# Softmax denominators of an attention and recurrence kernel: one group of four sums per two head pairs, divisors spread by transfers

## What is computed

```python
xn = _layernorm(x)
qkv = xn @ W_qkv + b_qkv                       # 16 heads of 64
scores = einsum('nqhd,nkhd->nhqk', q, k)
attention = softmax(scores / sqrt(64), axis=3)
out = einsum('nhql,nlhd->nqhd', attention, v).reshape(n, l, 1024) @ W_out + b_out
c = f * c + i * g                              # a gated recurrence over the 8 batches, on xn
h = tanh(xn @ wo.T + c_final @ uo.T + bo)
return x + out + h
```

## Time and profile before

| | |
|---|---|
| median of 3 runs | 908.32 us (907.5 to 911.02) |
| the profiled execution: its own time | 911.83 us |
| its span | 910.0 us |
| granted TensorE clock, mean | 0.979 |
| busy: PE, DVE, POOL, ACT | 96%, 63%, 60%, 49% |

### The profile page before, as it was taken

One profiled execution on the slowest core, in us unless ns is written; L12 is line 12 of the kernel. 1 busy time (PEld: TensorE's weight loads), 2 busy tenths in 40 slices (PEclk: granted clock), 3 DMA queues, 4 the chain that ended last, 5 costly groups with the idle time before them and its releaser, 6 DMA issues.

```text
span 910.0 us, 14933 instructions
## 1 busy us (share of the span) xinstructions
PE 875.1 (96%) x5429; PEld 554.0 (61%) x5429; DVE 571.1 (63%) x770; ACT 444.7 (49%) x579; POOL 548.2 (60%) x270
## 2 busy tenths in 40 slices
PE   4779999999999999999999999999999999999988
PEld 3545655655666666665666566665666566666643
DVE  6856666664766556665667476664766476665632
ACT  4335645652555555552555455552555355553531
POOL 4024644644777667773777677773777577774764
PEclk9669999999999999999999999999999999999999
DMA  7000000000100000000100000000100000000000
GB/s 232 1 0 1 9 17 0 1 13 1 36 2 13 0 1 34 0 12 0 35 0 12 0 23 12 0 12 0 35 0 12 0 23 12 0 13 1 13 13 12
DMA packets 18635, 13.75 MB, mean 15 GB/s; under 512 B 1298, under 2 KB 16176, under 8 KB 18608
## 3 DMA queue, kind: packets, MB, share of 16 engines
q1 hardware_dynamic: 18608, 13.39, 4.7%
HBM read 6.83 MB, written 2.10 MB: 10 GB/s over the span
## 4 chain that ended last, share of the span: by engine, by line
PE 89%; DVE 6%; ACT 2%; DMA 1%; issue 1%; SPq 1%; DVEq 0%
PE st L747 20%; PE pv L761 12%; PE misc L761 12%; PE st L689 9%; PE mx L728 8%; PE st L753 6%; PE mx L777 6%; PE mx L771 6%; PE pv L689 2%; DVE NM L507 2%; PE misc L673 2%; PE misc L689 2%; DMA probs<-in_L_attn_data_dram 1%; ACT probs L360 1%; DVE KL L493 1%; PE pv L673 1%
## 5 line engine op out<-in xcount | busy, mean ns | idle before, releaser
L507 DVE TENSOR_REDUCE NM<-mx 128x2 f32<-128x1024 f32 x256 | 313.8, 1226 | 172.7 <-PE mx L728 172.7
L360 ACT ACTIVATE probs<-st 128x1024 f32<-128x1024 f32 x256 | 257.3, 1027 | 93.9 <-PE st L753 88.7
L251 POOL TENSOR_TENSOR AT<-AT,RD 128x512 f32<-128x512 f32 x63 | 80.8, 1282 | 231.9 <-DVE RD L525 171.1
L259 POOL TENSOR_TENSOR PSUMK<-probs 128x1024 f32<-128x1024 f32 x64 | 153.4, 2397 | 99.5 <-ACT probs L360 99.5
L265 POOL TENSOR_TENSOR PSUMK<-PSUMK,probs 128x1024 f32<-128x1024 f32 x64 | 152.9, 2389 | 6.1
L272 POOL TENSOR_TENSOR PSUMK<-PSUMK,probs 128x1024 f32<-128x1024 f32 x64 | 152.8, 2387 | 6.1
L761 PE MATMUL misc<-probs,VALL 128*64 128x512 f32 x512 | 129.1, 593 | 0.9 <-DVE DL L472 0.9
L761 PE MATMUL pv<-probs,VALL 128*64 128x512 f32 x512 | 124.8, 607 | 0.7 <-DVE RES L478 0.7
L728 PE MATMUL mx<-KH,QH 64*128 64x512 f32 x512 | 112.4, 435 | 9.8 <-DVE NM L507 8.8
L747 PE MATMUL st<-QH,KH 64*128 64x512 f32 x512 | 107.4, 415 | 0.8 <-ACT probs L360 0.6
L747 PE MATMUL st<-QL,KH 64*128 64x512 f32 x512 | 101.5, 392 | 0.0
(11 more groups left out here) (179 smaller groups left out, 1240.5 us busy)
## 6 DMA issues: line engine op xcount, KB each, us to landing
probs<-in_L_attn_data_dram SPq DMA_DIRECT2D x4, 512.0 KB, 7.6
XSH<-XH SPq DMA_DIRECT2D x8, 256.0 KB, 2.4
XSL<-XL SPq DMA_DIRECT2D x8, 256.0 KB, 2.4
RES<-in_L_attn_data_dram SPq DMA_DIRECT2D x8, 256.0 KB, 2.8
out_dram<-RES SPq DMA_DIRECT2D x8, 256.0 KB, 2.3
probs<-in_L_attn_W_qkv_dram SPq DMA_DIRECT2D x3, 512.0 KB, 4.7
MROW<-TM SPq DMA_DIRECT2D x64, 4.0 KB
WO<-in_L_attn_W_out_dram SPq DMA_DIRECT2D x1, 512.0 KB, 4.8
```

The costliest lines, as they stand in the source:

```text
L251: nc.gpsimd.tensor_tensor(AT[:, s % PAIRS, :], AT[:, s % PAIRS, :], RD[:, s % 2, :], ALU.mult).then_inc(norm_done, 1)
L259: nc.gpsimd.tensor_tensor(PSUMK[:, s % 2, :, :], e[:, :, 0, :], e[:, :, 1, :], ALU.add).then_inc(sum_part, 1)
L360: nc.scalar.activation(probs[:, s % 2, :, u, :], st[:, u % 2, :, :], ACT.Exp, scale=SCALE).then_inc(exp_done, 1)
L507: nc.vector.tensor_reduce(NM[:, 0:4 * TB].rearrange("p (h a b) -> p h a b", h=2, a=2)[:, :, s % 2, b], mx[:, :, :], AX.X, ALU.max, negate= ...
```

## The change

- `sums` is called once per step, for both pairs. It makes four matmuls of 32 columns (`tile_position=(0, g)`), one head each in 32 partitions of the bank `st[:, 1, 1, :]`, and stands behind the second pair's values, in front of the next step's first maxima. In the last step it stands in front of the second pair's values. It waits for the POOL sums of both pairs and for DVE's `lo_k`, which reads that bank.
- DVE transposes the four heads' sums once into `RD[:, 0]` and takes one reciprocal into `R16`.
- SP copies the 16 columns of `R16` by six transfers into `RX`, so that each head's divisors stand in its 64 partitions, for both pairs.
- DVE fills `RD` from `RX` with one spreading transpose per pair in the next step, behind the fifth and the sixth of the eight reductions; the last step's fills come after its transfers.
- POOL normalises both pairs of the step before between its sums for the first and the second pair of the present one; before, one stood at the front and one at the end.
- PE no longer waits for the divisors' transpose before a step's first maxima, but before the scores of the first pair's second block, which use `st[:, 1]`.

```diff
+        RX = sb("RX", [P, 2, L // 32])
...
+            def spread_divisors(n, j):
+                sp.wait_ge(r16_done, STRETCHES * n + j + 1)
+                sp.sem_inc(passed_sp, 1)
+                for a in range(2):
+                    for to, of, count in ((0, 0, 32), (32, 0, 64), (96, 32, 32)):
+                        sp.dma_start(RX[to:to + count, a, :],
+                                     R16[HD * a + of:HD * a + of + count, :]).then_inc(d_r, 16)
...
                     for k in range(2):
-                        first_sum(t + k, s + k)
+                        first_sum(n, j, t + k, s + k)
                         second_sum(t + k, s + k)
                         third_sum(t + k, s + k)
-                    normalise(t, s)
+                        if k == 0 and not (first and j == 0):
+                            normalise(t - 2, s - 2)
+                            normalise(t - 1, s - 1)
...
+            def divisors(n, j):
+                dve.wait_ge(den_done, STRETCHES * n + j + 1)
+                wait(dve, norm_done, 8 * n + 2 * j)
+                nc.vector.transpose(RD[:, 0, :], st[:, 1, 1, :]).then_inc(den_used, 1)
+                dve.wait_ge(den_used, STRETCHES * n + j + 1)
+                wait(dve, d_r, 96 * (STRETCHES * n + j))
+                nc.vector.reciprocal(R16[:, :], RD[:, 0, :].rearrange("p (c j) -> p c j", j=32)[:, :, 0]).then_inc(r16_done, 1)
+            def fill_divisors(n, j, a):
+                dve.wait_ge(d_r, 96 * (STRETCHES * n + j + 1))
+                nc.vector.transpose(RD[:, a, :].rearrange("p (c j) -> p c j", j=32),
+                                    RX[:, a, :].unsqueeze(2).to_broadcast([P, L // 32, 32])).then_inc(rd_done, 1)
...
+            def sums(t):
+                pe.wait_ge(sum_done, t + 2)
+                for a in range(2):
+                    for h in range(2):
+                        g = 32 * (2 * a + h)
+                        last = nc.tensor.matmul(st[g:g + 32, 1, 1, :], ones[:, 0:32], PSUMK[:, a, h, :], start=True,
+                                                stop=True, tile_position=(0, g))
                 last.then_inc(den_done, 1)
...
-                    if coming:
-                        pe.wait_ge(red_done, 4 * (t + 4))
-                    sums(t, s, mx[:, 1, :])
...
                     pe.wait_ge(exp_done, 4 * t + 8)
+                    if not coming:
+                        sums(t)
+                    values(n, t + 1, s + 1)
                     if coming:
-                        values(n, t + 1, s + 1, (0, 1))
-                        pe.wait_ge(tm_done, STRETCHES * n + j + 2)
-                        sums(t + 1, s + 1, mx[:, 0, :])
-                        values(n, t + 1, s + 1, (2, 3))
-                    else:
-                        sums(t + 1, s + 1, st[:, 0, 0, :])
-                        values(n, t + 1, s + 1)
+                        if ahead:
+                            pe.wait_ge(k_lo, t + 6)
+                        sums(t)
```

More of the change, by code:

```diff
@@ L252, in normalise, with first_sum @@
                                         ALU.mult).then_inc(norm_done, 1)
-            def first_sum(t, s):
+            def first_sum(n, j, t, s):
                 pool.wait_ge(exp_done, 4 * t + 2)
-                wait(pool, den_done, t - 1)
+                wait(pool, den_done, STRETCHES * n + j)
                 e = probs[:, s % 2, :, :, :]
@@ L277, in step @@
                     s, t = 2 * j, 8 * n + 2 * j
-                    if not (first and j == 0):
-                        normalise(t - 1, s - 1)
                     for k in range(2):
-                        first_sum(t + k, s + k)
+                        first_sum(n, j, t + k, s + k)
                         second_sum(t + k, s + k)
                         third_sum(t + k, s + k)
-                    normalise(t, s)
+                        if k == 0 and not (first and j == 0):
+                            normalise(t - 2, s - 2)
+                            normalise(t - 1, s - 1)
             batches(pool, step)
+            normalise(8 * N - 2, PAIRS - 2)
         @block.scalar
@@ L605, in step @@
                     if coming:
-                        for b in range(TB - 1):
-                            maxima(t + 3, s + 3, b)
+                        maxima(t + 3, s + 3, 0)
+                    if not (first and j == 0):
+                        fill_divisors(n, j - 1, 0)
+                    if coming:
+                        maxima(t + 3, s + 3, 1)
+                    if not (first and j == 0):
+                        fill_divisors(n, j - 1, 1)
+                    if coming:
+                        maxima(t + 3, s + 3, 2)
                     if first:
@@ L627, in step @@
                         lo_state(s + 2)
[L628 to L629 removed]
+                    divisors(n, j)
             batches(dve, step)
+            fill_divisors(N - 1, 3, 0)
+            fill_divisors(N - 1, 3, 1)
             dve.wait_ge(pv_done, 8 * N)
@@ L857, in step @@
                         pe.wait_ge(tm_done, STRETCHES * n + j + 1)
-                        wait(pe, den_used, t)
+                        if first:
+                            wait(pe, t_done, 3 * s - 1)
+                        elif j == 1:
+                            pe.wait_ge(o_evac, n)
                         score_maxima(t + 2, s + 2, 0)
@@ L863, in step @@
                     if first:
+                        wait(pe, den_used, STRETCHES * n + j)
                         scores(n, t, s, 1, (0, 1, 2))
```

17 lines of the change are left out of this document (2 added, 15 removed).

## The result

| | before | after |
|---|---|---|
| median of the timed runs beside each other, us | 909.76 (906.76 to 911.49, 10 runs) | 914.68 (912.43 to 915.41, 10 runs) |
| profiled execution's span, us | 910.0 | 913.1 |
| granted clock, mean over the span | 0.979 | 0.975 |

The changed kernel is slower: the ratio is 1.0057, with a 95% interval from 1.0041 to 1.0073. The forecast was 0.8% slower.

The account below looks back on a forecast made before the run. PE, busy 96% of the span, was taken as the bound; steps -6.2 and +0.6, first batch +2.4 and tail +10.2 gave +7.0 us, so 915.3 against the 908.32 median, 0.8% slower, range 900 to 924.

Parts of the forecast that it names:

- Sums, "I take 0.86": PE's one group of four sums per step costs 0.86 us, plus 0.15 for tile-shape switching; gain 0.71 per step.
- two at a time: Rival on PE's sums: four strips run two at a time, the group takes 1.72 us, total 943; chance 6%.
- the estimate of 1.08: Rival on PE's sums: four strips cost 1.08 us and not 0.86, 7 us more, total 922; chance 8%.
- The first maxima, "loss 0.36 per step, say 0.4": At each seam PE's second maxima wait for DVE's late first reduction: 0.25 us plus 0.11 of open weight load.
- j = 1, "loss about 0.4, seven times": In later j = 1 steps the second pair's values wait for DVE's residual addition, no longer covered by sums.
- First batch, +2.4: First batch's four steps lose 0.15 us each, its three seams 0.6 each, since removing the first sums gains nothing there.
- the switch: Extra PE entry into and exit from the sums' tile shape, put at 0.15 us per step, between 0 and 0.3.
- POOL hides "by 0.3 to 0.7": POOL's sums and two normalisations end 20.9 us into the step, before PE asks, with 0.3 to 0.7 spare.
- Transfers: SP's six divisor copies take 4.1 us to issue, land after 5.5, and are hidden in the next step.
- Tail, +10.2: Last step grows 10.2 us: product wait 2.9, switch 0.15, half clock 0.8, late divisors 4.5, further clock and transposes 1.9.
- Sum: Whole execution: ordinary steps -6.2, j = 1 steps +0.6, first batch +2.4, tail +10.2, together +7.0 us.
- The late reduction costs nothing: Rival at the seams: DVE's late first reduction does not delay PE; steps of 22.2 us, total 902.7; chance 22%.

Follow-up runs that it names:

- The last kernel: Changed kernel plus reciprocal behind the first reduction, earlier residual addition, last step's old divisors and reordered values, product and sums; 892.32 us, ratio 0.9804 to the kernel before.

## Why the prediction was right

The sign, the size (0.8% forecast, 0.57% measured) and the range held, and the likeliest case was the one that came: one cheap group, a first reduction that comes late, and a long tail. The mechanisms are shown by the experiments. That the size fits so well is in part luck, since several terms were off in both directions. By its steps:

- *Sums, "I take 0.86".* Right. The group is one row of eight records in two bunches 0.45 apart (0.48 foreseen), and costs 0.99 up to the next maxima (1.01 foreseen). The last kernel shows the whole gain with the losses removed: 0.64 to 0.79 a step, 0.71 foreseen. The two rivals in which four strips cost more (two at a time, or the estimate of 1.08 from the Trainium skill, "TensorE: Matmul & The Clock Gate", section on packing small matmuls) would have made it 1.85 or 1.21. This trace shows no price for the third and the fourth strip.
- *The first maxima, "loss 0.36 per step, say 0.4".* The mechanism is right, and that the second maxima wait for DVE is shown by doubling and by moving the reciprocal. The size was off both ways. At the written-out seams it is 0.22: the sum had the reduction start at 1.15 and last 1.23, and it started at 1.06 and lasted 1.17, since it begins 0.08 before the reciprocal's record ends. At the loop's own seam it is 0.77: the gap of 0.42 on DVE was not foreseen. In the kernel before, the last instruction there was a spreading transpose of 0.7 us, which covered it, and the change left a reciprocal of 0.25 in its place. The mean over a looped batch, (3 x 0.22 + 0.77) / 4 = 0.36, is the number that was worked out, by two errors that cancel in this mean.
- *j = 1, "loss about 0.4, seven times".* Right: with the residual addition earlier, 0.35 came back.
- *First batch, +2.4.* Measured +2.1, but not by its terms. The second pair's values do wait the 0.86 more that the first sums covered (1.09 and not 0.23). The late reduction was put at 0.6 at each of three seams; moving the reciprocal gave back 0.20 to 0.27 there, so it was put at more than twice its price. What remained, 0.27 to 0.30 a step, is twice the 0.15 that was put for the switch, and no run shows why. The seam into the loop, measured +0.59, had only 0.15 in this term, and 0.42 of it was the reciprocal.
- *POOL hides "by 0.3 to 0.7".* It hides by 0.8. The run with the sums between the values shows how little that is: asked 1.9 earlier, POOL's chain is what PE waits for.
- *Transfers.* Hidden in the steps: the six are issued from 449.40 in the step from 448.16, and the first fill starts at 457.68, directly behind a reduction. Six issues take 3.76 and not 4.1, and in the last step the fill starts 4.85 after the first issue (897.07 to 901.92), where 5.5 was put.
- *Tail, +10.2.* Measured +10.7 for the last step itself. The product came 2.7 late and not 2.9, its half clock cost 1.7 where half of that (0.8) was put, and the end product came 9.20 after the sums, where 9.8 was put.
- *Sum.* +7.0 was forecast on the profiled execution, and the spans differ by 3.1. Of the missing 3.9, 1.3 is the start's scatter, 0.3 the first batch, and 2.8 the ends of the 27 later steps, for which the sum had -5.6 and the marks show -8.4 (-7.8, and -0.6 in front of the last step); the tail gives 0.5 back. The term that was mis-sized there is "say 0.4", which counts 27 x 0.4 = 10.8. What was lost is 20 x 0.22 at the written-out seams, 5 x 0.77 at the loop's and 0.36 at its exit, 8.6 in all; the 27th seam leads into the last step, which has no maxima to delay. An ordinary step is 22.47 long, below the forecast's 22.6 to 22.7 and above the rival's 22.2.
- *"The late reduction costs nothing".* The rival had no share. Its condition, DVE free before 0.9 into the step, is met only with the reciprocal behind the first reduction, where the reduction starts 0.78 to 0.83 into the step, and there an ordinary step is what the rival had said (22.27, against its 22.2).

What stays open: why a written-out seam loses 0.22, the loop's exit 0.36 and the way into the loop 0.42 with the same instructions. At the first, the reduction's record begins 0.08 before the reciprocal's ends; at the other two it begins behind it, and its length is 1.23 and not 1.17. That accounts for the difference, but no run shows what makes it. Open is also what the first batch's steps lose beside the reciprocal.

## What to carry to other kernels

When work on the bounding engine moves to the end of a step, look at what its reader has queued in front of that engine's next need: here a reciprocal of 0.25 us in the wrong place cost a third of the gain at a written-out seam and all of it at the loop's own, and moving it behind one reduction gave that back. Let the last instruction before a loop's branch be a long one on an engine that is awaited right behind it; that was seen on DVE here, and on no other engine. Merge work in the steady state and keep the old form in the last step, where a latency that other steps hide stands in the open: the last step cost 10.7 us here, against the 8.4 that all step ends behind the first batch gained.

## What the runs showed of the hardware

- Four matmuls of 32 columns each, with 512 moving columns of 32-bit floats, cost PE nearly what two of 64 columns do: 0.99 from the group's start to the next maxima, against 0.86 and 0.10 for the exit. The four strips start together, and their second records 0.45 later.
- On DVE the loop's way back takes 0.65 to 0.69 us, counted from the start of the last instruction before it, so 0.40 to 0.44 stand in the open behind a reciprocal of 0.25, and nothing behind a transpose of 0.72.
- A reduction on DVE can begin 0.08 us before the record of the instruction ahead ends (449.22 against 449.30); here it did not use that one's result.
- The clock's price is that of the work behind a hole: after 3.40 us in which PE was busy for 0.89, twelve matmul records took 7.11 in place of 5.42.
